# Scores over all 128 rows with zeroed rows 96 to 127; transposed output first in the DMA queue, second load of the rows last

## The reference

```
xn = layernorm(x)                                   # over the 256 columns, eps 1e-5
q, k, v = split(xn @ Wqkv.T), 16 heads of 16;  q *= 16 ** -0.5
# segments of 512 rows; keys and values are every 8th row: 64 per segment
scores = q4 @ k4.T                                  # per head and segment: 512 x 64
c   = max(scores) over blocks of 64 queries, per key
w   = exp(scores - c);  den = sum(w, keys) + 1e-10;  att = (w @ v) / den
ffn = relu(xn @ W1 + b1) @ W2 + b2                  # 256 -> 1024 -> 256
out = x + att @ Wout.T + ffn
```

## Time and profile before

| | |
|---|---|
| median of 3 runs | 1069.88 us (1069.55 to 1072.47) |
| profiled execution | 1070.42 us, of which 1068.6 us span |
| TensorE busy | 1046.8 us, 98% of the span |
| VectorE, ScalarE, GpSimd busy | 76%, 61%, 58% |
| DMA | 216 MB, 72.5% of the 16 engines' span on SyncE's queue |
| granted TensorE clock | 0.999 |

### The profile page before, as it was taken

How to read it: one execution, slowest core, us unless ns; L and a number is a source line. 1 busy time by engine, 2 the same in 40 slices (tenths; PEclk the granted TensorE clock), 3 DMA queues, 4 the chain that set the end, 5 groups by cost and what they waited for, 6 DMA issues and landing times.

```text
span 1068.6 us, 19173 instructions
## 1 busy us (share of the span) xinstructions
PE 1046.8 (98%) x5381; PEld 811.4 (76%) x5381; DVE 817.3 (76%) x1465; ACT 648.3 (61%) x1080; POOL 622.3 (58%) x487
## 2 busy tenths in 40 slices
PE   6999999999999999999999999999999999999998
PEld 4677787777787777777777877777877777877777
DVE  7877877877878777778778778778777778787753
ACT  5656665666656566565666656666666665656663
POOL 4355565656656656556655656566565565556564
PEclk9999999999999999999999999999999999999999
DMA  5457777777776878777777777778778687767744
GB/s 192 98 155 210 223 213 207 195 213 220 223 213 179 224 201 232 221 195 198 207 223 223 215 208 197 217 214 229 213 192 216 197 236 212 211 175 218 194 144 145
DMA packets 153576, 216.38 MB, mean 202 GB/s; under 512 B 27344, under 2 KB 96720, under 8 KB 153552
## 3 DMA queue, kind: packets, MB, share of 16 engines
q1 hardware_dynamic: 153408, 215.96, 72.5%
q10 hardware_dynamic: 144, 0.13, 0.0%
HBM read 100.41 MB, written 58.46 MB: 149 GB/s over the span
## 4 chain that ended last, share of the span: by engine, by line
PE 84%; DMA 6%; DVE 4%; SPq 3%; issue 2%; ACT 0%; DVEq 0%
PE h_bank L1023 36%; PE y_bank L1023 36%; PE s_banks L1096 5%; PE misc L1203 3%; PE s_banks L1203 2%; DMA k_dram<-k_lo 2%; PE misc L1023 2%; DMA yt_dram<-y_mem 1%; DVE xn L824 1%; DMA xt_dram<-z 1%; DMA k_pack<-k_dram 1%; SPq L406 1%; DVE s_max L841 1%; SPq L428 1%; DMA x_raw<-x 1%
## 5 line engine op out<-in xcount | busy, mean ns | idle before, releaser
L533 POOL TENSOR_TENSOR h_lo<-h_full,h_hi 128x512 fp32r<-128x512 f32 x256 | 336.1, 1314 | 382.2 <-ACT h_full L614 378.8
L620 ACT ACTIVATE w_exp<-w_exp 128x512 f32<-128x512 f32 x256 | 161.6, 632 | 241.8 <-DVE w_exp L847 240.2
L612 ACT ACTIVATE h_hi<-h_bank,b_cols 128x512 fp32r<-128x512 f32 x256 | 174.5, 682 | 70.2 <-PE h_bank L1023 63.4
L1023 PE MATMUL h_bank<-xt_hi,w_hi 128*128 128x512 f32 x512 | 206.4, 403 | 0.0
L1023 PE MATMUL h_bank<-xt_lo,w_hi 128*128 128x512 f32 x512 | 200.2, 391 | 0.0
L1023 PE MATMUL h_bank<-xt_hi,w_lo 128*128 128x512 f32 x512 | 199.7, 390 | 0.0
L841 DVE TENSOR_REDUCE s_max<-s_banks 128x8 f32<-128x512 f32 x254 | 170.9, 673 | 34.5 <-PE s_banks L1096 34.5
L1023 PE MATMUL y_bank<-h_hi,w_hi 128*128 128x512 f32 x496 | 194.7, 392 | 0.2 <-ACT w_exp L620 0.2
L1023 PE MATMUL y_bank<-h_lo,w_hi 128*128 128x512 f32 x496 | 193.9, 391 | 0.0
L1023 PE MATMUL y_bank<-h_hi,w_lo 128*128 128x512 f32 x496 | 193.6, 390 | 0.0
L847 DVE TENSOR_TENSOR w_exp<-s_banks,s_max 128x512 f32<-128x512 f32 x254 | 175.7, 692 | 11.0
(11 more groups left out here) (139 smaller groups left out, 1509.4 us busy)
## 6 DMA issues: line engine op xcount, KB each, us to landing
q_pack<-q_hi SPq DMA_DIRECT2D x248, 128.0 KB, 2.5
rden_rows<-rden_dram SPq DMA_DIRECT2D x128, 128.0 KB, 4.6
x_b<-x SPq DMA_DIRECT2D x32, 512.0 KB, 4.5
x_raw<-x SPq DMA_DIRECT2D x31, 512.0 KB, 4.8
q_pack<-q_lo SPq DMA_DIRECT2D x124, 128.0 KB, 2.4
yt_dram<-y_mem SPq DMA_DIRECT2D x124, 128.0 KB, 3.6
y_mem<-yt_dram SPq DMA_DIRECT2D x31, 512.0 KB, 4.7
out<-x_b SPq DMA_DIRECT2D x31, 512.0 KB, 3.1
```

The lines of the kernel that those rows point to most:

```text
L533: pool.tensor_tensor(h_part[1][:, i % HBUF], h_full[:, i % HBUF], f32(h_part[0][:, i % HBUF]), ALU.subtract).then_inc(h_lo, 1)
L612: act.activation(h_part[0][:, i % HBUF], h_bank[i % 2][:], ACT.Relu, bias=b1_cols[:, i:i + 1]).then_inc(h_hi, 1)
L620: act.activation(w_exp[:, pair], w_exp[:, pair], ACT.Exp).then_inc(w_ready, 1)
L1023: mm = pe.matmul(ps, stationary[a], moving[b], start=start and c == 0 and n == 0, stop=stop and c == len(pairs) - 1 and n == 2, skip_group ...
```

## The change

The score matmul reads all 128 partitions of `k_pack` and `q_pack`. GpSimd sets partitions 96 to 127 of both to zero at the start of the program, and TensorE waits for that before the first such score. On SyncE's queue the order of a step is another: `y_to_dram` first, `y_from_dram` ahead of `transposed_in`, and `load_again` at the end. GpSimd's `residual` stands four hidden tiles later.

```
--- before.py
+++ after.py
@@ -202,6 +202,7 @@
         pair_packed = [sem(f"pair_packed{j}") for j in range(PAIRS // 2)]
         k_out = sem("k_out")
         k_packed = sem("k_packed")
+        pack_zeroed = sem("pack_zeroed")
         v_ready = sem("v_ready")
         k_hi = sem("k_hi")
         k_lo = sem("k_lo")
@@ -456,10 +457,14 @@
                 sp.dma_start(out_rows[s], x_b2[:, par]).then_inc(y_stored[par], 16)
 
             def step(s, par, ffn, attention, norm, load):
+                if ffn and later(s):
+                    y_to_dram(s - 1)
                 if norm and not by_tensor(s):
                     blocks_to_dram(s)
                 if ffn:
                     rden_to_dram(s)
+                if ffn and later(s):
+                    y_from_dram(s - 1)
                 if norm and not by_tensor(s):
                     transposed_in(s)
                 if isinstance(s, int) and s == 0:
@@ -473,12 +478,6 @@
                     load_keys(s + 3)
                 if ffn and not (isinstance(s, int) and s == 0):
                     rden_spread(s)
-                if ffn and later(s):
-                    y_to_dram(s - 1)
-                if ffn and not by_rows(s):
-                    load_again(s, par)
-                if ffn and later(s):
-                    y_from_dram(s - 1)
                 if norm:
                     keys_to_dram(s)
                     pack(s, 0)
@@ -494,6 +493,8 @@
                     pack(s, 3)
                 if ffn and later(s):
                     store(s - 1, 1 - par)
+                if ffn and not by_rows(s):
+                    load_again(s, par)
                 if attention and not norm:
                     load_again(s + 1, 1 - par)
                 if by_rows(s):
@@ -513,6 +514,11 @@
             pool.wait_ge(identity_zero, 1)
             pool.affine_select(out=identity[:], in_=identity[:], compare_op=ALU.not_equal, fill=1.0,
                                base=0, pattern=[[-1, P]], channel_multiplier=1).then_inc(consts_made, 1)
+            pool.wait_ge(consts_made, 3)
+            pool.memset(f32(k_pack[PR:P]).rearrange("p j c n -> p (j c n)"), 0.0).then_inc(pack_zeroed, 1)
+            pool.wait_ge(pack_zeroed, 1)
+            pool.memset(f32(q_pack[PR:P]).rearrange("p n t -> p (n t)"), 0.0).then_inc(pack_zeroed, 1)
+            pool.wait_ge(pack_zeroed, 2)
 
             def inverse_deviation(s, par):
 
@@ -558,9 +564,9 @@
                 for i in range(LAG, NH):
                     if i in first:
                         hidden_lo(past(s), first[i])
-                    if i == 2 and ffn and later(s):
+                    if i == (4 if by_rows(s) else 6) and ffn and later(s):
                         residual(s - 1, 1 - par)
-                    if i == 3 and by_rows(s):
+                    if i == 5 and by_rows(s):
                         residual(s, par)
                 if attention and ffn:
                     for quad in range(QUADS):
@@ -1093,7 +1099,9 @@
                     pe.wait_ge(num_den_ready, past((s + 1) * QUADS))
                     pe.wait_ge(k_packed, (s + 1) * K_PACKED)
                 pe.wait_ge(s_shifted, past((s + 1) * PAIRS + n - 1))
-                pe.matmul(s_bank[n % 2], k_pack[0:PR, pair % (PAIRS // 2), pair // (PAIRS // 2)], q_pack[0:PR, pair], start=True,
+                if isinstance(s, int) and s == 0 and n == 0:
+                    pe.wait_ge(pack_zeroed, 2)
+                pe.matmul(s_bank[n % 2], k_pack[:, pair % (PAIRS // 2), pair // (PAIRS // 2)], q_pack[:, pair], start=True,
                           stop=True).then_inc(s_psum, 1)
 
             def first_scores(group, queries_made, shifted):
```

More of the change, by code:

```diff
@@ L475, in step @@
                     rden_spread(s)
[L476 to L481, removed]
                 if norm:
```

1 line of the change is left out of this document (added).

## The result

The changed kernel takes 1212.74 us (median of 6, 1195.51 to 1222.08) against 1069.72 us for the kernel before on the same chip (1066.97 to 1072.47). The ratio is 1.123, 95% interval 1.118 to 1.127. The prediction said 1075 us, in a range of 1060 to 1086. Three of the six executions took 1195 to 1207 us and three 1218 to 1222; the ratio is made from the first three, and the profiled execution (1222.08 us, span 1220.3) is one of the others, so I read single steps from it more than its total. Lines are counted in the changed program: the splits of the transposed rows L651 and L880 are now L657 and L886, the products L1023 are L1029, and the load of the rows L434 is L435.

A forecast was written before the change was run, and what follows sets the result against it. TensorE, busy throughout the step examined, was taken as the bound. From 1070.4 us: + 11.7 (stalls) + 1 (program end) - 4.3 (key waits) - 3.6 (scores) = 1075.2, less 0.5 for the median: 1075 us, range 1060 to 1086.

The forecast's parts named there:

- the scores' excess: On TensorE, a score over 96 rows costs about 0.028 us more than a 128-row matmul; 3.6 us gained in even steps.
- the zeroing: GpSimd's memsets at the start, 4.2 us, fit into its 5.39 us idle gap and cost nothing.
- The waits for packed keys: TensorE's five waits for packed keys vanish because the keys' store goes out earlier; 4.3 us gained.
- The rule by which a late row becomes a stall: ScalarE's split of the rows 1.65 us late, less 0.8 us of slack, stalls TensorE 0.9 us ahead of the queries.
- stall, odd and even step: TensorE stalls 0.9 us in each odd step, 13 times, 11.7 us in all; nothing in even steps.
- Its landing takes 3.7 us (median): The load of the transposed rows still lands 3.7 us after issue: 545.0 in place of 542.4 in the odd step.
- The blocks start 2.6 us later: On SyncE's queue in the odd step, new issues ahead delay the blocks' store, and so the rows' load, by 2.6 us.
- my ceiling of 2.9: Upper bound in us for the blocks' delay in the odd step, from the added transfer time; the floor was 1.7.
- Nothing lost, with 0.9 us to spare: In the even step queue slack limits the delay to 1.1 to 1.9 us; rows land before ScalarE needs them.
- The residual add falls into the 2.80 us for which GpSimd waits: The moved add on GpSimd, 2.44 us, fits its wait ahead of the last hidden tile and costs nothing.
- The attention's wait for the reciprocals' rows: These rows move by about 2.6 us behind the rows' load; costed at nothing, up to 1.7 us an odd step otherwise.
- the last wait at the end of the program: The last reciprocals' rows go out behind the last transposed output's store and load; about 1 us lost.

The follow-up runs named there:

- e1: The kernel before with only the zeroing and the scores over 128 rows; 1067.7 us, ratio 0.9989, not told from no change.
- e7: e1 with GpSimd's residual add alone moved to where the change puts it, queue as before; 1104.03 us, ratio 1.032.
- e2: The changed kernel with the scores back over 96 rows; 1211.91 us, ratio 1.135.
- e3: The changed kernel with the load back of the transposed output moved behind the load of the transposed rows; 1114.19 us, ratio 1.044.
- e6: The changed kernel, but the rows' load is issued only when the load back of the transposed output has landed; 1200.05 us, ratio 1.121.
- e10: e1 with the store of the transposed output ahead of the store of the transposed rows' blocks, nothing else moved; 1070.43 us, ratio 1.0014.
- e5: e1 with the second load of the input rows last in the step and the residual add behind hidden tile 4; 1072.6 us, ratio 1.0025.
- e9: e6 with 16 (odd step) or 9 (even step) extra matmuls in TensorE's stall, their results overwritten; 1163.16 us, ratio 1.089.

## Why the prediction was wrong

Right were the scores' excess (e1, though a step gained less by it than was counted), the zeroing, and the direction: TensorE waits for the rows. The waits for packed keys ended too, but e7, whose queue is as before, has none either, so the reason given for it is not shown. The rule by which a late row becomes a stall was right too. It said that TensorE loses what ScalarE is late, less 0.8 us. Over 13 odd steps, from the third step on, the rows land at 22.65 us and ScalarE began at 16.7 in e1: 5.95 less 0.8 is 5.1, and the queries are 66.5 / 13 = 5.1 us later. For the 13 even ones behind them, 21.9 less 18.7, less 0.8, is 2.4, and 31.0 / 13 = 2.4 was measured. (In e2 the queries are 89 us later over these 26 steps than in the kernel before, which also has scores over 96 rows; here 97.5.) What went into that rule was wrong.

| term | predicted | measured |
|---|---|---|
| issue of the rows later, odd step | 2.6 us | 3.4 |
| the same, even step | 1.1 to 1.9 | 3.2 |
| issue to landing | 3.7 | 7.1 (median) |
| stall, odd and even step | 0.9 and 0 | 5.1 and 2.4 |
| clock after the stall | no term | 43.8 us in 26 steps |
| residual add on GpSimd | 0 | 35 us alone (e7), covered in the changed kernel |

**"Its landing takes 3.7 us (median)": the step that failed most.** I moved the issue and kept the landing, although the change puts a load of 512 KB directly ahead of it. With 3.8 us to the landing and the measured issue, the rule gives 15.6 + 3.8 - 16.7 - 0.8 = 1.9 us in an odd step (e3, whose rows land so, has 1.7) and 15.8 + 3.8 - 18.7 - 0.8 = 0.1 in an even one, some 26 us over these 26 steps. The measured stalls are 97.5, so some 72 us of them are the longer landing, in most steps that of one engine. e3 and e6 take it away in two ways. The Trainium skill (DMA: Bandwidth & Descriptors, section Queues, rings and completion order) states that each DMA engine consumes its descriptors in ring order, and that an engine's part of the semaphore is written only after its earlier writes. The trace agrees in that the rows count as landed with the last of 16 reports, at 8.0 us where the 15th came at 4.4. That the rows come late when the load back is still under way at their issue is shown; why one engine of 16 falls behind, after the load back has landed and in 20 of 29 steps only, no run shows.

**"The blocks start 2.6 us later", and L434 "moves" with them.** The store alone moves the rows by 1.8 us (e10), the second load at the end of the list alone by 1.9 us (e5: 17.9 in place of 16.0 in the odd step), and both together by 3.3 (e3). I had counted the second load as one issue of 0.4 us, and the blocks' time from first issue to landing as unchanged: the blocks start 3.0 us later in the changed kernel and take some 0.3 more to land, above my ceiling of 2.9 in all.

**"Nothing lost, with 0.9 us to spare" in the even step.** I let the queue's slack hide the new issues up to the blocks' store, which does start only 1.6 us later there, and left out that the blocks then take longer too: 5.5 us from their first issue to their landing in place of 3.9. So the rows are issued 3.2 us later, and with their longer landing this makes 31 us in 13 steps.

**No term for the clock.** I priced a stall at its length. In the changed kernel these 26 steps grow by 141.3 us against e1 and the queries are late by 97.5; the other 43.8 are matmuls at the lower level after the stalls. In e6 the same two numbers are 116.3 and 79.7, and in e9, where TensorE doesn't idle, the steps grow by 79.6: just the stall. So this part is shown for e6; for the changed kernel, which was not run with filled stalls, it is read from the granted clock of 0.52 after the stall.

**"The residual add falls into the 2.80 us for which GpSimd waits": nothing.** It did fall there; but GpSimd waits just while VectorE splits the rows, and the add slows VectorE down. In the changed kernel it costs nothing, because the rows come after the add is over (L886 takes 688 ns in the median there). Where the rows come in time it costs some 35 us (e7). I had asked what hides it on its own engine, and not what runs beside it.

The attention's wait for the reciprocals' rows, costed at nothing, is 14.2 us in 13 waits of GpSimd, after the stall; the last wait at the end of the program grew from 10.2 to 13.8 us, where 1 was estimated.

## What to carry to other kernels

When a load that ends a critical path gets another transfer directly ahead of it, ask again for its landing, not only for its issue, and for the last of its 16 engines. On a kernel whose TensorE is always busy, ask what a stall does to the matmuls after it: here they ran at the lower clock level, which cost 44 us beside 97 of stalls, while e3, with 1.7 us of stall in an odd step, kept a clock of 0.995. Before an instruction is put into idle time of GpSimd, look at what VectorE does in that time.

## What the runs showed of the hardware

- A matmul over 96 rows of the contraction stood 0.028 us longer than one over 128 with 512 columns; with 32 zeroed rows added the excess was gone.
- A subtraction of VectorE with two inputs in SBUF took 1.8 us in place of 0.69 beside GpSimd's add and split.
- One of 16 DMA engines landed its part of a 512 KB load up to 3.6 us after the other 15, where another load of 512 KB was still under way when it was issued; where that had landed before the issue, all 29 loads landed within 3.6 to 4.2 us.
- After 3.7 us without a matmul the granted clock of the step fell to 0.91; with 16 matmuls that do nothing useful in that time it stayed at 1.00, and the program, with such matmuls in every stall, was some 35 us shorter.
